# Moving six weight-rounding jobs and two weight splits to other steps of a hand-scheduled attention and feed-forward kernel

## The reference, cut to what matters

```
def _quantized_matmul(x, w, scale):
    wq = w.astype(jnp.float8_e4m3fn).astype(x.dtype)
    y = jnp.einsum('bsi,io->bso', x, wq)
    return y * scale
gate = silu(_quantized_matmul(x, gate_w, gate_scale))      # x: 64x256, gate_w: 256x768
up = _quantized_matmul(x, up_w, up_scale)                  # up_w: 256x768
ffn = _quantized_matmul(gate * up, down_w, down_scale)     # down_w: 768x256

x = x + tanh(g_xattn[0]) * xattn(layernorm(x), ctx, ...)   # 16 heads of 128, 4 key/value groups, 64 context + 64 own keys
x = x + tanh(g_ffn[0]) * ffn(layernorm(x), ...)
```

## Time and profile before

| | |
|---|---|
| median of 3 runs | 309.91 us |
| the profiled execution, its own time | 310.24 us |
| its span, first to last instruction | 308.0 us |
| PE busy | 294.0 us (95%) |
| DVE, ACT, POOL busy | 231.3, 232.1, 183.4 us (75%, 75%, 60%) |
| granted TensorE clock, mean | 1.00 |
| DMA | 12.84 MB, nearly all of it in the first tenth of the span |

### The profile page before, as it was taken

One profiled execution on the slowest core, in us unless ns is written; L12 is line 12 of the kernel. 1 busy time (PEld: TensorE's weight loads), 2 busy tenths in 40 slices (PEclk: granted clock), 3 DMA queues, 4 the chain that ended last, 5 costly groups with the idle time before them and its releaser, 6 DMA issues.

```text
span 308.0 us, 6587 instructions
## 1 busy us (share of the span) xinstructions
PE 294.0 (95%) x2243; PEld 235.3 (76%) x2243; DVE 231.3 (75%) x482; ACT 232.1 (75%) x893; POOL 183.4 (60%) x178
## 2 busy tenths in 40 slices
PE   7898989998999999999999999999999999988876
PEld 3345666666877888888888888888888888877865
DVE  1768997899899987879864876768765975686553
ACT  2586889977879788998887778787887678776632
POOL 1446685677648695567755685457746684556230
PEclk9999999999999999999999999999999999999999
DMA  6999000000000010001000010000000000000001
GB/s 198 388 390 397 24 17 2 0 1 10 11 3 1 2 34 2 0 2 36 2 0 2 0 37 0 3 0 20 2 1 2 0 19 2 2 0 19 0 0 36
DMA packets 6720, 12.84 MB, mean 42 GB/s; under 512 B 800, under 2 KB 4256, under 8 KB 6688
## 3 DMA queue, kind: packets, MB, share of 16 engines
q1 hardware_dynamic: 6688, 12.43, 11.3%
HBM read 11.38 MB, written 1.05 MB: 40 GB/s over the span
## 4 chain that ended last, share of the span: by engine, by line
PE 28%; ACT 28%; DVE 26%; issue 8%; POOL 5%; DMA 2%; SPq 1%; DVEq 0%; POOLq 0%
ACT probs L950 11%; ACT squares L785 6%; PE ps_y L446 4%; DVE row_max L1245 4%; DVE exp_bias L1248 4%; DVE q_sin L1109 4%; DVE q_rot L1105 3%; ACT qt L869 3%; PE ps_attn L752 3%; PE ps_scores L704 3%; ACT const L842 2%; PE ps_transposed L432 2%; PE ps_kv L420 2%; DMA q_raw<-in_wq_dram 2%; PE ps_probs L432 2%
## 5 line engine op out<-in xcount | busy, mean ns | idle before, releaser
L950 ACT ACTIVATE probs<-ps_scores,exp_bias,q_scale 128x128 f32<-128x128 f32 x128 | 56.9, 455 | 23.7 <-DVE exp_bias L1248 23.6
L1426 POOL TENSOR_TENSOR q_rot<-q_rot,q_sin 128x512 f32<-128x512 f32 x31 | 40.0, 1292 | 18.4 <-DVE q_sin L1109 18.1
L1470 POOL TENSOR_TENSOR probs<-probs,row_inv 128x512 f32<-128x512 f32 x32 | 36.2, 1133 | 17.9 <-DVE row_inv L1304 17.8
L1377 POOL TENSOR_TENSOR q_scale<-ssq_eps,minus_half 128x4 f32<-128x4 f32 x32 | 39.8, 1244 | 10.6 <-DVE ssq_eps L1274 9.6
L1388 POOL TENSOR_TENSOR fuse_lo<-fuse,fuse_hi 128x256 fp32r<-128x256 f32 x21 | 15.4, 733 | 41.3 <-ACT fuse_hi L794 41.3
L785 ACT ACTIVATE squares<-ps_q 128x128 bf16<-128x128 f32 x128 | 34.1, 292 | 5.8 <-PE ps_q L414 4.1
L752 PE MATMUL ps_attn<-pt,values 128*128 128x256 f32 x128 | 33.4, 383 | 0.0
L704 PE MATMUL ps_scores<-kt,qt 128*64 128x128 f32 x512 | 33.3, 273 | 0.0
L926 ACT ACTIVATE pt<-ps_probs 128x512 f32<-128x512 f32 x32 | 19.2, 600 | 13.3 <-PE ps_probs L432 13.3
L704 PEld LDWEIGHTS ps_scores<-kt,qt 128*64 128x64 f32 x512 | 28.9, 137 | 0.0
L1105 DVE TENSOR_TENSOR q_rot<-ps_q,rope 128x512 f32<-128x512 f32 x31 | 21.3, 686 | 9.7 <-ACT squares L785 9.7
(11 more groups left out here) (195 smaller groups left out, 839.2 us busy)
## 6 DMA issues: line engine op xcount, KB each, us to landing
q_raw<-in_wq_dram SPq DMA_DIRECT2D x4, 512.0 KB, 8.3
o_raw<-in_wo_dram SPq DMA_DIRECT2D x4, 512.0 KB, 12.3
ctx_t<-in_ctx_dram SPq DMA_DIRECT2D x8, 128.0 KB, 2.7
out_dram<-x_sb SPq DMA_DIRECT2D x8, 128.0 KB, 1.7
stage<-in_gate_w_dram SPq DMA_DIRECT2D x2, 384.0 KB, 10.1
stage<-in_up_w_dram SPq DMA_DIRECT2D x2, 384.0 KB, 11.1
x_sb<-in_x_dram SPq DMA_DIRECT2D x1, 768.0 KB, 13.1
stage<-in_down_w_dram SPq DMA_DIRECT2D x2, 384.0 KB, 13.1
```

The source lines that it names most:

```text
L950: last = nc.scalar.activation(probs[:, i, :], ps_s[:, i * P:(i + 1) * P], ACT.Exp, bias=exp_bias[:, i:i + 1], scale=q_scale[:, k % 2, i:i ...
L1377: return nc.gpsimd.tensor_tensor(dst, src, minus_half[:, 0:src.shape[1]], ALU.pow)
L1426: nc.gpsimd.tensor_tensor(q_rot[:, :, :], q_rot[:, :, :], q_sin[:, :, :], ALU.add)\
L1470: nc.gpsimd.tensor_tensor(probs[:, :, :], probs[:, :, :], row_inv[:, :].unsqueeze(2).broadcast_to([P, 4, P]), ALU.mult).then_inc(probs_rea ...
```

## The change

Three tables of step numbers change and nothing else. The rounding of chunks 0 to 5 moves from steps 0, 1, 2, 3, 4 and 7 to steps 1, 2, 3, 4, 5 and 6. The spreading of the flag moves from step 4 to step 5 and `down_row_scale` with it from step 5 to step 6. The splits of query group 0 (step 5) and of query group 1 with kv 0 (step 6) move to steps 6 and 7. ACT's conversions and POOL's stores follow their chunks: the conversions from steps 1 to 4 to steps 2 to 5, the stores from steps 5 and 8 to steps 6 and 7. The amount of work is the same.

```
-SPLIT_AT = {5: [("q", 0)], 6: [("q", 1), ("kv", 0)], 8: [("q", 2), ("kv", 1)], 9: [("q", 3), ("kv", 2)], 10: [("kv", 3)],
+SPLIT_AT = {6: [("q", 0)], 7: [("q", 1), ("kv", 0)], 8: [("q", 2), ("kv", 1)], 9: [("q", 3), ("kv", 2)], 10: [("kv", 3)],
...
-ROUND_AT = {0: 0, 1: 1, 2: 2, 3: 3, 4: 4, 7: 5}
-NAN_AT = 4
+ROUND_AT = {1: 0, 2: 1, 3: 2, 4: 3, 5: 4, 6: 5}
+NAN_AT = 5
```

## The result

The changed kernel takes 316.44 us (median of 4 runs, 316.18 to 317.12), the kernel before 309.95 in the same comparison: ratio 1.0209, 95% interval 1.0197 to 1.0222, so 6.5 us slower. The profiled execution took 316.18 us with a span of 314.1.

The account below looks back on a forecast made before the run. The prediction took PE, busy 294.0 of 308.0 us, to bound the kernel. Its terms -1.2 + 1.3 + 4.9 - 0.3 + 1.1 gave +5.8 us on the 309.91 us median, so 315.7 us, range 313.1 to 318.6.

Parts of the forecast that it names:

- Step 0: Without the rounding in step 0, k_var starts earlier and PE turns step 1's keys sooner: 1.2 us gained.
- Step 5: Chunk 4's rounding replaces a split ahead of xn on DVE, so PE gets xn later: 1.3 us lost.
- Step 6: PE's first feed-forward piece newly waits for row scale L1085, now behind row_inv: 4.9 us lost, bounds 3.5 to 7.0.
- I take half of the 0.7 more: In step 6, POOL's k_sin beside the first rounding piece was counted at half its possible 0.7 us slowdown.
- both hindrances: POOL's w_down delaying exp_bias and k_sin delaying the rounding piece in step 6; in full, 5.3 us for this step.
- Steps 7 and 8: Group 1's split beside w_down loses 0.1 us, step 8's idle PE piece goes for 0.4: 0.3 us gained.
- The clock: After step 6's wait PE returns at 1.2 GHz for 2.3 us: 1.1 us lost, ends 0 and 2.5.
- The sum: All terms together for the whole kernel: +5.8 us, so 315.7 us.
- (a): The clock does not fall behind step 6's wait and the rest stands: +4.7, 314.6 us; chance 0.25.
- (b): POOL's hindrances add up, step 6 at 7.0, step 5 at 2.0, clock low longer: +10, 319.9 us; chance 0.08.
- (c): DVE freed early: 3.5 at step 6, 0.6 at step 5, no clock fall: +2.6, 312.5 us; chance 0.13.
- (d): PE does not set the end, step 6's wait is swallowed, only gains count: -1.6, 308.3 us; chance 0.04.

Follow-up runs that it names:

- Experiment 7: Kernel before with chunk 0's rounding in step 0 cut to 8 of its 768 columns; 309.00 us, ratio 0.9965.
- experiment 1: Kernel before with only the spreading of the flag and the row scale L1085 moved one step later; 314.62 us, ratio 1.0136.
- experiment 2: Changed kernel with the row scale L1085 put ahead of the row maximum of step 6; 312.67 us.
- experiment 3: Changed kernel with the row scale L1085 between the split and the first rounding piece of step 6; 312.58 us.
- experiment 6: Changed kernel with L1085 ahead of step 6's row maximum, plus 11 matmuls on constants ahead of PE's wait for xn; 312.64 us.
- experiment 4: Changed kernel with 20 matmuls on constants ahead of PE's wait for the row scale in step 6; 314.52 us.
- experiment 5: Changed kernel with 20 matmuls on constants ahead of PE's row-scale wait and 11 ahead of its xn wait; 314.84 us.
- experiment 8: Changed kernel with L1041 and L1050 of chunk 4's rounding in step 5 cut to 8 of 768 columns; 315.93 us.
- experiment 11: Kernel before with peak reductions of chunks 0 and 1 done in step 3 and L1085 moved just behind xn; 309.12 us.
- experiment 12: Kernel before with chunk 0 and 1 peaks in step 3, L1085 behind xn, step 0's row_inv between L1028 and L1031; 308.96 us.

## Why the prediction was right, point by point

- **Step 0, -1.2 us: right.** 1.33 us in the profile, 0.12 of it from an earlier start of the whole; -1.2 from the row maximum of step 0 on. Experiment 7 shows it alone. What the prediction put at nothing stayed so: PE's lead is 1.33 us at 27.08 and 1.38 at 65.48 (before, 66.86), with all conversions and the matmuls of L515 between. Its list of idle pieces leaves out a wait of 0.84 us for the probabilities at 44.91; the change left it as it was (0.84 at 43.57).
- **Step 5, +1.3 us: right, 0.2 high.** PE turned xn 1.08 us later than the gain of step 0 would have it, with a wait of 2.04 us for the 2.2 forecast. L1050 took its full 1.28 us and xn 0.40, as forecast. (70.88 + 0.41 is 71.29 and not 71.25, which changes nothing.)
- **Step 6, +4.9 us: right in place and cause, half a microsecond low.** PE lost 5.45 us between the turn of xn and the first feed-forward piece. The step that fell short is "I take half of the 0.7 more": k_sin held L1028 up for 0.85 us. The sum with both hindrances in full, which stood beside it as the Trainium skill's exclusive lock ("SBUF — State Buffer", "SBUF: two separate sides"), was 5.3 and nearer. The wait shows as only 3.71 us, less than the 4 to 6 that the prediction gave as its sign, since PE had come 1.74 us late to it by the first slow stretch.
- **Steps 7 and 8, -0.3 us: right, 0.3 us too little gained.** The split of step 7 took 2.83 us beside w_down, and the turn-to-projection path lost 0.07; from there to the projection of step 9 PE gained 0.66, not 0.40 (102.21 for 96.18, 6.03 behind).
- **The clock, +1.1 us: the direction right, the reasoning too simple.** The second fall cost 1.42 us (3.23 us from the piece to the next turn of queries, 1.81 before); runs with and without a fall put it at 1.4 to 2.1. The prediction took the time at half speed from the time that the fall took, 2.3 us; no row showed it, and it was about 3.1 or more. It also missed that there would be two falls, and that the first would be free.
- **The sum**, +5.8, stands against 6.03 us at step 9 of the profiles and 6.5 between the medians. That it is so close to the profiles is in part luck: 0.5 too little at the wait and 0.3 at the clock met 0.1 too little gained in step 0, 0.2 too much lost in step 5 and 0.3 too little gained in step 8. The other half microsecond is in which executions were profiled.
- **The rivals.** (a), no fall, did not come true in any of the four runs, though in experiment 1 a wait of 3.2 us went without a fall in two runs of six. (b) was right only in that both hindrances of step 6 counted in full; its slow split (1.22 us, not 2.86) and slow xn (0.40, not 1.09) did not come. (c) fell with the 5.45 us of step 6, and (d) too: PE's delay of 6.04 us at step 10 is that of the end.

One thing the prediction left unsaid: putting the row scale earlier won back 3.8 us and no more, and 2.7 us stayed lost (experiments 2, 3 and 6). The long wait hid that VectorE and POOL come late in steps 6 to 8 once it is gone. How much of the 2.7 us belongs to this schedule and how much to the new places of L1085, where it took 1.97 and 1.13 us for 0.39, no run separates.

## What to carry to other kernels

When a job moves to another step, list every semaphore that it raises and ask who waits for it in the step where it now ends; here one small instruction behind row_inv cost more than all six moved roundings won. Price a VectorE instruction by what POOL does beside it in the new place, in full. And before removing a wait, ask what is late just behind it: here 2.7 us stayed lost without the long wait, with the slow clock and without it.

## What the runs showed of the hardware

The price of a fall of the clock depends on what stands behind it: 1.4 to 2.1 us where PE sets the pace (experiments 1, 4 and 5), nothing where a later wait absorbs it (experiments 2, 4, 5 and 6). Whether it falls is not settled by the length of a wait alone: behind the wait of 2.0 us for xn the clock was at half in the profiles of the changed kernel and of experiments 2, 3 and 4, but one run of each of these three experiments had a mean clock of 1.000 with the same code up to there; a wait of 3.16 us went without a fall, and behind the 0.90 us at the same place before there was none. Matmuls on constants in the long wait kept the clock up and made the program 1.9 us faster; in the shorter wait they brought nothing.

VectorE instructions that met a POOL instruction on 128x512 or 128x768 could last until POOL's was done, whatever their own size: exp_bias on 128x4 took 1.14 us and ended with w_down, and one on 128x8 took 1.00 us and ended with POOL's probabilities (68.34 and 68.31), where its neighbour of the same size took 0.17. So shortening or reordering VectorE work there moved the delay from one instruction to the next (experiments 8, 11, 12).
